# Depthwise convolutions as 22x4 to 16x2 patches on TensorE, and a preparation that queues its loads at once

## The reference

```
# layer 0: two selective-scan blocks over the 4096 pixels, then a 1x1 map and a batch norm
seq = seq + mamba_block(seq)                    # twice
out = fus_w[:, :C] @ mamba_out + fus_w[:, C:] @ gp + fus_b        # gp: relu(gp_w @ mean(x) + gp_b), per image
x0  = (out - mean(out)) * rsqrt(var(out) + EPS) * bn_g + bn_b + x # mean, var over images and pixels
# layer 1: group norm (32 groups of 3 channels, per image), three depthwise kernels, a 1x1 map
h   = (x0 - group_mean(x0)) / sqrt(group_var(x0) + EPS)
x3, x5, x7 = dwconv3x3(h) + b3, dwconv5x5(h) + b5, dwconv7x7(h) + b7    # 'SAME', one kernel per channel
x1  = x0 + wf @ concat(x3, x5, x7) + bf
# layers 2 and 3: attention and an MLP over the channels of every pixel
```

## Time and profile before

| what | value |
|---|---|
| median of three runs | 4350.67 us |
| the profiled execution's own time | 4347.45 us |
| its span | 4345.6 us |
| mean granted TensorE clock | 0.918 of full speed |
| busy PE / DVE / ACT / POOL | 85% / 77% / 55% / 66% of the span |
| DMA | 607.50 MB, mean 140 GB/s |

### The profile page before, as it was taken

How to read it: one execution, slowest core, us unless ns; L and a number is a source line. 1 busy time by engine, 2 the same in 40 slices (tenths; PEclk the granted TensorE clock), 3 DMA queues, 4 the chain that set the end, 5 groups by cost and what they waited for, 6 DMA issues and landing times. The chain is left out here.

```text
span 4345.6 us, 39976 instructions
## 1 busy us (share of the span) xinstructions
PE 3674.2 (85%) x11136; PEld 1703.6 (39%) x11136; DVE 3347.4 (77%) x3962; ACT 2373.1 (55%) x3961; POOL 2852.7 (66%) x2326
## 2 busy tenths in 40 slices
PE   6899999999999999999999999987129988685766
PEld 2333333333333333333333333332029985463554
DVE  4999999999999999999999999999320004656565
ACT  5667666667666667666667666665121101425334
POOL 4988999988999988999988999988100000203123
PEclk8999999999999999999999999999569998777666
DMA  3555555555555555555555555555564456100000
GB/s 89 180 160 166 164 166 162 175 169 165 164 165 162 177 168 164 168 161 162 178 168 163 168 162 163 175 160 170 134 163 145 147 146 154 31 15 15 15 1 29
DMA packets 246461, 607.50 MB, mean 140 GB/s; under 512 B 56496, under 2 KB 90419, under 8 KB 245087
## 3 DMA queue, kind: packets, MB, share of 16 engines
q1 hardware_dynamic: 210654, 535.73, 41.9%
q10 hardware_dynamic: 35584, 69.23, 5.7%
HBM read 553.77 MB, written 72.56 MB: 144 GB/s over the span
## 5 line engine op out<-in xcount | busy, mean ns | idle before, releaser
L785 POOL TENSOR_TENSOR prod<-states,c_rows 128x512 f32<-128x512 f32 x1536 | 1922.7, 1272 | 176.9 <-DVE states L715 142.7
L715 DVE TENSOR_TENSOR_SCAN states<-decay,carry,bpsum 128x512 f32<-128x512 f32 x1344 | 1677.2, 1259 | 0.0
L444 PE MATMUL ypsum<-prod,identity 128*128 128x512 f32 x3072 | 1593.7, 602 | 0.5 <-POOL prod L785 0.3
L550 ACT ACTIVATE decay<-delta,decay_rate 128x512 f32<-128x512 f32 x1344 | 934.7, 711 | 312.5 <-DVE states L715 308.2
L695 DVE TENSOR_TENSOR bpsum<-bpsum,dx 128x512 f32<-128x512 f32 x1344 | 904.6, 673 | 138.5 <-PE bpsum L437 124.3
L1596 POOL TENSOR_TENSOR y<-y,b 128x384 f16<-128x384 f16 x64 | 66.4, 1038 | 1072.3 <-ACT y L1419 1072.3
L444 PEld LDWEIGHTS ypsum<-prod,identity 128*128 128x128 f32 x3072 | 583.3, 194 | 422.4 <-issue 283.4
L437 PE MATMUL bpsum<-b_rows,select 96*128 96x512 bf16 x1344 | 522.0, 389 | 211.8 <-DVE states L715 209.3
L437 PEld LDWEIGHTS bpsum<-b_rows,select 96*128 96x128 bf16 x1344 | 129.4, 96 | 974.3 <-DVE states L715 690.7
L1020 PE MATMUL convp<-image,band_w 128*128 128x252 f32 (+3 forms) x1440 | 334.2, 395 | 19.2 <-DMA image<-normed_map 19.2
L1020 PEld LDWEIGHTS convp<-image,band_w 128*128 128x128 f32 x1440 | 332.7, 325 | 20.4 <-issue 19.2
(11 more groups left out here) (184 smaller groups left out, 4486.3 us busy)
## 6 DMA issues: line engine op xcount, KB each, us to landing
c_rows<-bc_map SPq DMA_DIRECT2D x512, 512.0 KB, 3.9
c_rows<-bc_map SPq DMA_DIRECT2D x512, 256.0 KB, 4.1
b_wide<-bc_map ACTq DMA_DIRECT2D x128, 256.0 KB, 4.7
band_rows<-tap_bands SPq DMA_DIRECT2D x64, 360.0 KB, 5.6
band_w<-band_rows SPq DMA_DIRECT2D x96, 240.0 KB, 3.9
depthwise_map<-dw_sums ACTq DMA_DIRECT2D x48, 384.0 KB, 4.4
dw_parts<-depthwise_map SPq DMA_DIRECT2D x16, 1152.0 KB, 7.7
b_wide<-bc_map ACTq DMA_DIRECT2D x128, 128.0 KB, 4.2
```

The lines of the kernel that those rows point to most:

```text
L444: pe.matmul(ypsum[:, group % Y_BANKS, :], identity[:, :], prod[:, n % P_RING, :], start=s == 0, stop=s == STATES - 1).then_inc(summed, 1)
L550: act.activation(into, delta[k % 2][:, g, :], ACT.Exp, scale=decay_rate[:, ORDER[k][0], g, s:s + 1]).then_inc(done, 1)
L715: dve.tensor_tensor_scan(states[:, n % H_RING, :], by, add, carry[:, at, u:u + 1], ALU.mult, ALU.add).then_inc(scanned, 1)
L785: pool.tensor_tensor(prod[:, n % P_RING, :], states[:, n % H_RING, :], c_rows[:, n // C_STATES % C_RING, n % C_STATES, :], ALU.mult).then_ ...
```

## The change

What changes, by stage:

- **Scan stage.** The table of taps is smaller (9 columns x 37 rows x 3 kernels a channel in place of 128 x 15), and 16 transfers in steps 0 to 15 write `patch_rows` (88 x 96 x 2 x 96 numbers) in runs of 48 numbers, in place of 64 transfers in runs of 960.
- **Preparation.** `load_all` and its barrier go. SyncE queues four small constants, then maps, then the other twelve constants and the first weights; `x0` holds all four images, and its stores move into the convolution stage, after channels 12, 32, 52 and 72. VectorE multiplies the fused map by its scale in the same instruction that adds `x0`; the shift is added to the statistics and, in the last stage, to the bias, so ScalarE's scaling pass goes. ScalarE normalises into `padded`: even and odd columns apart, 4 blocks of 22 rows, with zeros at the edges, in six instructions an image; the map is stored by two transfers an image, in runs of 140 numbers.
- **Convolutions.** One channel at a time. A patch of 22 rows and 4 columns gives 16 rows and 2 columns of all three kernels: 88 inputs to 96 outputs. The columns of the tile are 4 images x 4 row blocks x 32 column pairs = 512. The 4 columns are two pairs, so a channel takes two products (`t` = 0 and 1) with one image tile of 88 partitions, read two columns apart. The image is loaded by two transfers of 44 partitions, the weights of 4 channels by one of 88 partitions. ScalarE copies 96x512 and stores it in runs of 128 numbers.
- **Last stage.** Groups are 4 rows of each of the 4 blocks. `parts` is loaded in two runs of 1536 numbers a channel, `x0_group` in four of 256; VectorE's addition becomes two instructions of 512 columns, one for even and one for odd columns; the output is stored in runs of 256 numbers in place of 512.

```diff
-TAP_AT, TAPS_ALL = (0, 3, 8), 15
-SPREAD_AT = (9, 13)
+ROW_BLOCKS, BLOCK_ROWS, EDGE = 4, 16, 3
+PATCH_ROWS, HALF_SIDE = BLOCK_ROWS + 2 * EDGE, SIDE // 2
+HALF_ROW = HALF_SIDE + EDGE
+PATCH, PATCH_OUT = 4 * PATCH_ROWS, 2 * BLOCK_ROWS * len(SIDES)
+TAP_ROWS, TAP_COLS = PATCH_ROWS + BLOCK_ROWS - 1, 9
+SPREAD_AT = 9
...
-                def spread_bands(row):
-                    sp.dma_start(dram["band_rows"][:, row, :, :].rearrange("c m j -> c (m j)"),
-                                 tap_dram[:, SIDE - 1 - row:2 * SIDE - 1 - row, :].rearrange("c m j -> c (m j)")).then_inc(bands_spread, 16)
+                def spread_taps(i):
+                    q, co = divmod(i, 2)
+                    t, at = divmod(q, 4)
+                    width, kinds = BLOCK_ROWS * len(SIDES), len(SIDES)
+                    window = bass.AP(tap_dram.tensor, ((q + 1 - co) * TAP_ROWS + PATCH_ROWS - 1) * kinds,
+                                     [[TAP_COLS * TAP_ROWS * kinds, C], [-kinds, PATCH_ROWS], [1, width]])
+                    sp.dma_start(dram["patch_rows"][PATCH_ROWS * at:PATCH_ROWS * (at + 1), :, t, width * co:width * (co + 1)]
+                                 .rearrange("r c m -> c r m"), window).then_inc(bands_spread, 16)
...
+                    def load_patches(j):
+                        if j >= W_RING:
+                            sp.wait_ge(conv_done, W_CHANNELS * (j - W_RING + 1))
+                        sp.dma_start(patch_w[:, j % W_RING, :, :, :].rearrange("p c t m -> p (c t m)"),
+                                     dram["patch_rows"][:, W_CHANNELS * j:W_CHANNELS * (j + 1), :, :]
+                                     .rearrange("p c t m -> p (c t m)")).then_inc(patch_loaded[j % W_RING], 16)
+                    def load_image(c):
+                        if c >= I_RING:
+                            sp.wait_ge(conv_done, c - I_RING + 1)
+                        for e in range(2):
+                            flat = image[2 * PATCH_ROWS * e:2 * PATCH_ROWS * (e + 1), c % I_RING, :, :].rearrange("p n i -> p (n i)")
+                            sp.dma_start(flat[:, 0:LINE - 1], img_dram[c, :, e:LINE - 1 + e]).then_inc(image_loaded[c % I_RING], 16)
...
+                    for b in range(2, BATCH):
+                        sp.wait_ge(x0_added, b - 1)
+                        load_f(b)
+                        if b + 1 < BATCH:
+                            load_x(b + 1)
+                    for tile, src in rest:
+                        sp.dma_start(tile, src).then_inc(rest_loaded, 16)
+                    for j in range(W_RING):
+                        load_patches(j)
                     for b in range(BATCH):
-                        sp.wait_ge(x0_added, b + 1)
-                        sp.dma_start(x0_dram[:, b, :], x0[:, b % 2, :]).then_inc(x0_stored, 16)
-                        sp.wait_ge(norm_ready, b + 1)
-                        sp.dma_start(img_dram[:, :, b, :], work[:, b % 2, :].rearrange("c (h w) -> c h w", w=SIDE)).then_inc(img_stored, 16)
...
+                        for phase in range(2):
+                            sp.wait_ge(norm_ready, 2 * b + phase + 1)
+                            sp.dma_start(img_of[:, phase, :, b, :],
+                                         padded[:, b % 2, phase, :, :, :].rearrange("c r n i -> c r (n i)")).then_inc(img_stored[b % 2], 16)
...
+                        for t in range(2):
+                            last = pe.matmul(banks[0:PATCH_OUT, c % 4, :].rearrange("m (n i) -> m n i", i=HALF_SIDE),
+                                             patch_w[:, j % W_RING, c % W_CHANNELS, t, :],
+                                             image[:, c % I_RING, :, 2 * t:2 * t + HALF_SIDE], start=t == 0, stop=t == 1)
...
+                        act.activation(sums[:, c % O_RING, :, :], banks[0:PATCH_OUT, c % 4, :].rearrange("m (b n) -> m b n", b=BATCH),
                                        ACT.Copy).then_inc(evicted, 1)
+                        act.dma_start(dw_dram[c, :, :, :].rearrange("b m n -> m b n"),
+                                      sums[:, c % O_RING, :, :]).then_inc(sums_stored[c % O_RING], 16)
...
-                        dve.wait_ge(f_scaled, b + 1)
-                        dve.tensor_tensor(x0[:, b % 2, :], x0[:, b % 2, :], work[:, b % 2, :], ALU.add).then_inc(x0_added, 1)
+                        dve.wait_ge(fx_loaded[b], 32)
+                        dve.scalar_tensor_tensor(x0[:, b, :], fmap[:, b % 2, :], scale0[:, :], x0[:, b, :],
+                                                 ALU.mult, ALU.add).then_inc(x0_added, 1)
```

More of the change, by code:

```diff
@@ L955, in _ @@
                 def _(sp):
-                    def load_bands(p):
-                        if p >= W_RING:
-                            sp.wait_ge(conv_done, p - W_RING + 1)
-                        for a in range(2):
-                            half = slice(SIDE * a, SIDE * a + SIDE)
-                            sp.dma_start(bands[half, p % W_RING, half, :].rearrange("h m j -> h (m j)"),
-                                         dram["band_rows"][2 * p + a, :, :, :].rearrange("h m j -> h (m j)")).then_inc(bands_loaded[p % W_RING], 16)
@@ new lines, in _ @@
+                    for i in range(2):
+                        sp.wait_ge(img_stored[i], 32 * BATCH // 2)
+                    for c in range(I_RING):
+                        load_image(c)
+                    for c in range(C):
+                        if c % W_CHANNELS == W_CHANNELS - 1 and c // W_CHANNELS + W_RING < C // W_CHANNELS:
+                            load_patches(c // W_CHANNELS + W_RING)
+                        if c + I_RING < C:
+                            load_image(c + I_RING)
+                        for b in due(X0_STORE_AT, c):
+                            sp.dma_start(x0_dram[:, b, :], x0[:, b, :]).then_inc(x0_stored, 16)
@@ L1035, in normalise @@
                         act.wait_ge(gn_ready, b + 1)
-                        act.activation(work[:, b % 2, :], x0[:, b % 2, :], ACT.Identity, scale=small[:, b, 6:7],
-                                       bias=small[:, b, 7:8]).then_inc(norm_ready, 1)
+                        act.wait_ge(zeroed, 1)
+                        if b >= 2:
+                            act.wait_ge(img_stored[b % 2], 32 * (b // 2))
+                        rows = x0[:, b, :].rearrange("c (n r w) -> c r n w", n=ROW_BLOCKS, w=SIDE)
+                        scale, bias = small[:, b, 6:7], small[:, b, 7:8]
+                        for phase in range(2):
+                            cols = slice(1 - phase, SIDE, 2)
+                            into = padded[:, b % 2, phase, :, :, 2 - phase:2 - phase + HALF_SIDE]
+                            act.activation(into[:, EDGE:EDGE + BLOCK_ROWS, :, :], rows[:, :, :, cols], ACT.Identity, scale=scale, bias=bias)
+                            act.activation(into[:, 0:EDGE, 1:, :], rows[:, BLOCK_ROWS - EDGE:, :ROW_BLOCKS - 1, cols], ACT.Identity,
+                                           scale=scale, bias=bias)
+                            act.activation(into[:, EDGE + BLOCK_ROWS:, :ROW_BLOCKS - 1, :], rows[:, 0:EDGE, 1:, cols], ACT.Identity,
+                                           scale=scale, bias=bias).then_inc(norm_ready, 1)
+                    act.wait_ge(first_loaded, 16 * len(first))
                     act.wait_ge(gp_full, 1)
@@ L1117, in _ @@
                     dve.wait_ge(sums_ready, 1)
+                    dve.wait_ge(first_loaded, 16 * len(first))
                     dve.wait_ge(gp_ready, 1)
@@ L1218, in batch_phase, with rows_of @@
                         fills[kind, p, c] = len(fills)
+        def rows_of(tensor, b, row, count):
+            return tensor[:, b, :].rearrange("c (n r w) -> c n (r w)", n=ROW_BLOCKS, w=SIDE)[:, :, row * SIDE:(row + count) * SIDE]
         with nc.Block() as block:
```

233 lines of the change are left out of this document (110 added, 123 removed).

## The result

The changed kernel takes 4302.35 us (median of 4 runs, 4297.15 to 4304.14), the kernel before 4350.77 (4 runs, 4346.25 to 4351.54): a ratio of 0.9889, 95% interval 0.9872 to 0.9906. The forecast was 4196 with a range from 4140 to 4255; it missed by 106 us, and the range does not hold the time. The profiled execution took 4304.14 us, with a span of 4302.3.

The account below looks back on a forecast made before the run. The prediction took transfers and their order to bound the preparation and TensorE alone the convolutions. From 4347.45, -0.8 - 42 - 114 + 2 gave 4192.6; with the median 3.2 above the profile, 4196 us, range 4140 to 4255.

Parts of the forecast that it names:

- the first of the convolution stage: Convolution stage: TensorE needs 0.90 us a product, two products a channel, 172 us for 96 channels against 334.
- Scan stage: Scan stage: GpSimd's smaller clearing saves 0.8 us; the 16 patch transfers cost 0, with -1 to +15 kept.
- Preparation: Preparation: bound by transfers and their order, it falls from 168.5 to 126.8 us, a gain of 42.
- The two side cases of the forecast: Preparation: gain 28 with stores at 201 GB/s and 10 us of gaps, 64 at 257 without the 97 rows.
- Convolution: Convolution stage: transfers take over as the bound and need 220 us, 2.3 us a channel, a gain of 114.
- Transfers at 230 GB/s: Convolution stage: 50.6 MB of images, results, weights and `x0` stores move at 230 GB/s, taking 220 us.
- Last stage: Last stage: VectorE's addition as two instructions pays a fixed part twice, 0.2 us each time; +2 us in all.
- Few engines: Convolution stage: loads of 44 and 88 rows use 11 engines, not 16; 270 us, kernel 4246; chance 0.19.
- TensorE as the bound: Convolution stage: transfers keep up and TensorE's 172 us set the time, kernel 4148; chance 0.14.
- The clock falls: Convolution stage: a third of the channels run at half clock, 262 us, kernel 4238; chance 0.10.
- Late scan units: Scan stage: units come late behind 192-byte runs, 2 us in each of 16 steps, kernel 4228; chance 0.04.
- paid packets: Convolution stage: each packet costs 138 ns whatever its size, 422 us in place of 220, kernel 4398; chance 0.03.

Follow-up runs that it names:

- e8: e1 with the four `x0` stores moved behind the last image load: 4174.76 us.
- e9: e7 with the three constants of 97 rows each loaded as 96 rows and one row apart: 4172.65 us.
- e12: e1 with the 97-row constants loaded as 96 rows and one, and each `x0` store cut in four: 4149.58 us.
- e1: The changed kernel with 8 rows of zeros added to image and weight tiles, so products have 96 rows: 4178.52 us.
- e13: e12 with the last stage's two additions of 96x512 a group made one of 96x1024: last stage 784.4 us, after 792.2.
- e7: The changed kernel with 24 rows a quarter (two of zeros), so 96-row products and loads of 48 and 96 partitions: 4182.78 us.
- e2: The changed kernel with products padded to 128 rows (40 of zeros) and 128 columns of weights: 4175.38 us.
- e6: The kernel before, with its depthwise products reading 88 of their 128 rows: 4609.99 us.
- e10: The changed kernel (88 rows) with twelve 128-row products ahead of the convolutions and the `x0` stores behind the last image load: 4179.66 us.
- e16: e12 with products reading 96 rows in channels 0 to 7 and 88 from channel 8 on: 4232.05 us.
- e5: The changed kernel (88 rows) with twelve products of 128 rows and 128 columns right ahead of the first channel's product: 4289.82 us.

## Why the prediction was wrong, step by step

**The step that failed** is the first of the convolution stage: "TensorE: the last stage's products have the same 512 columns in FP32, and 12 records (6 products) take 5.39 us, 0.90 a product", hence 172 us for TensorE and the transfers as the bound. The group has 96x96 products at full clock. The price of a product was taken with its clock, as if the clock were part of the shape. With 88 rows, entered at 0.50, the clock stayed at 0.50 and TensorE alone took 328 us. With 96 rows it takes 172.6 us of busy time in e8: the arithmetic was right for a shape that the change does not have.

**The sum, term by term.**
- *Scan stage*, -0.8: measured -0.35. The wide runs of the patches delayed no unit.
- *Preparation*, -42: measured -49. The first store was issued 68.5 us after the first load (2 + 66.5 in the sum), which is luck: the sum had the wait of the 97-row loads behind this point, and it lies ahead of it. From there to the first product 50.9 us, not 58.3. The 9.9 us for the 97-row loads were about right in size: apart they give 11.4 us (e9), 11.9 between the medians. But their wait stands in SyncE's issues ahead of the stores, not in the stores' parts on one engine. The two side cases of the forecast come out at gains of 27 and 65 us, not 28 and 64, which changes nothing. ScalarE's last copy for an image ended at 3164.3 us, 17 before the first product, so a transfer was last, as forecast; but ScalarE had first waited 28.0 us in one piece for a buffer of `padded` to be stored, which the forecast thought covered.
- *Convolution*, -114: measured -6. The other 108 us are nearly the whole miss; the other terms (-7 and +10) nearly cancel.
- *Transfers at 230 GB/s*: not the bound here (151 GB/s), and too low where they might be: e12 moves 263 GB/s in its stage. With the clock up, the `x0` stores between image loads cost 27 us (e1 against e8). That is what the forecast's "they cost their bytes" gives (6.3 MB at 230 GB/s, 27 us), but for another reason: cut in quarters, the same bytes cost 5. With 96 rows and the stores cut, the stage is 187 us, nearer to TensorE's 172 than to 220.
- *Last stage*, +2: measured +12.3. The fixed part of the second instruction was right (0.206 us, forecast 0.2), but what it delays was not worked out: some 7 us in all by e13.

**The rivals.** Few engines: out (e7 against e1 and e2). TensorE as the bound: right in kind, with half the clock. The clock falls: the right cause at 0.10, but mis-sized, since it looked at how busy TensorE would be and let a third of the channels run slow; here TensorE was busy all the time and all 96 ran slow. Late scan units and paid packets: out. The forecast "I am wrong in the size if TensorE shows no waits" came true, with 327 in place of 172.

**What the profile of before could have told.** TensorE entered the stage at 0.50 and had 0.99 within it, with 128 rows; no product around the change had 88. So the clock of the new shape was an unknown cost, whose bounds are 172 and 344 us (twice), and the range should have held both ends.

## What to carry to other kernels

Price a matrix product by its time and its granted clock together, and where a change makes a whole stage of products with fewer rows than those that the trace shows raising the clock, bound its time by both levels of the clock. If a stage of such products shows 0.50 without a gap, pad the rows with zeros to a whole 96 (here 88 to 96 took 118 of 328 us away, for two memsets). Cut large stores that share a queue with just-in-time loads, and load a 97-row constant that stands behind large loads as 96 rows and one.

## What the runs showed of the hardware

- FP32 products of 88, 90, 92, 94 and 95 rows with 512 numbers never raised the granted clock from 0.50 in up to 328 us without a gap; 96 and 128 rows raised it each time. Products of 88 rows with 244 to 256 numbers left it at 0.50 for 602 us (e6). The number of columns (96 or 128) did not matter, and zeros in the added rows were enough. Products of 12 and 64 rows between larger ones ran at 1.00 in the scan stage.
- A full clock, once there, is held by 88 rows: 175 us in e10, some 50 us in e16, until a gap. In e5 it ended at a gap of 3.8 us, in e16 at the second of two gaps of 0.8 to 0.9 us close together.
- A record of an 88x512 product follows the last by 0.854 us at 0.50, and by 0.443 (7.09 us for 16) at 1.00.
- A 97-row load behind another one, with maps queued ahead, held the issuing queue for 16.07 us; a load of 96 rows and one of one row took 0.64 us for the pair. Without maps ahead the same 97-row load took 0.61 us.
- In the preparation a VectorE instruction on 96x4 numbers took 4.97 us, where its neighbours took 0.16, and ended when GpSimd's clearing of `padded` did (3061.99 + 10.39 = 3072.38). The timeline (start, length) of the changed kernel:

```profile
3061.99 10.39 POOL L1178 MEMSET padded<- 96x6160 f32 x2 [11.52 <-POOLq L850]
```

VectorE at that time:

```profile
3067.25 0.15 DVE L1156 TENSOR_SCALAR gpt<-gpt 96x1 f32<-96x1 f32 x1
3067.43 4.97 DVE L1157 TENSOR_SCALAR gpt<-gpt 96x4 f32<-96x4 f32 x1
3072.44 0.16 DVE L1158 TENSOR_TENSOR gpt<-gpt 96x4 f32<-96x4 f32 x1
```

That the one held the other up is read from the times alone; no run took the clearing away.
